# A fused two-attention block: chunks of 128 tokens split into halves of 64, with a state between the halves

## The chip, the cores and the metric

One core of a Trainium2 chip runs the whole program. The metric is the time of one execution in microseconds, the median of the runs.

## The reference, cut to what matters

The input is 4 sequences of 2048 tokens with 512 channels, in float32. Four layers follow one another, each on a layer-normalised copy of x, and each added to x:

```python
x = x + attn_a(layernorm(x))      # causal linear attention, 16 heads of 64
x = x + ffn(layernorm(x), rhs)    # x quantised by rows, rhs by columns, 512x512
x = x + attn_b(layernorm(x))      # gated decaying state, 16 heads, rank 16 x 32
x = x + ffn(layernorm(x), rhs)
```

Attention A takes q = relu(x Wq) + 0.001 and k = relu(x Wk) + 0.001; for each head, the output at token t is q_t times the sum over all tokens up to t of k v, divided by q_t times the sum of k; then Wo and a bias. Attention B turns q and k by a rotary table, projects them by head to rank 16, gates k by a sigmoid, and for each head keeps a 16x32 state M with M = M * decay + k v and y = q M; then an output projection, a residual and a layernorm of its own. Both are sums over all earlier tokens, so they can be worked in chunks: what came before a chunk is a state, and what lies inside it is a masked score matrix.

## The kernel before, in words

**Tiling.** The 8192 tokens are 64 chunks of 128 tokens. A chunk passes through all four layers. Sums over the tokens before a chunk are kept in `state_a` (eight pairs of heads, 64 rows for each head of a pair, 64 columns and one for the sum of k) and in `state_b` (32 rows for each pair of heads).

**Steps.** The kernel is a list of some 95 steps for a chunk, `ORDER`, with a lag for each. The body of the loop is one slot: in slot s a step with lag l works on chunk s - l, and every engine walks the list in this order and does the steps that are its own. So each engine's queue is fixed by the list, up to six chunks are in flight (the largest lag is 5), and engines meet at semaphores only. The first slots, before the loop, also hold the pieces that load, scale and split the weights (`LATE` says after which step), and the last slots drain the pipeline. `BANK` gives each PSUM result one of 8 banks; a bank has a semaphore for full and one for empty, and a step that takes a bank waits until the last user's copy out of it is done.

**TensorE's steps.** Projections are three f16 passes (`three_pass`, L752 to L754: high by high, high by low, low by high): `qk0` to `qk3`, `v0`, `v1`, `wo0`, `wo1`, `qb`, `kb`, `vb`, `gb`, `qr`, `kr`. `mm0` and `mm1` are the two ffn products (L917), `out` is the f32 output projection of attention B (L1038), `kt0`, `kt1`, `kT` are f32 transposes by an identity (L710). The rest are f32 matmuls on parts of the 128x128 array:

- `s0`, `s1` (L832): scores k q of attention A, in blocks of 64 keys by 64 queries, one quarter of the array each. Of the four blocks of a 128x128 score matrix three are computed: the two on the diagonal and the one below it. Places of the halves are swapped for some heads (`key_half`, `query_half`), so that the two row halves of the array have equal work.
- `so0`, `so1` (L847): the queries times `state_a`, started into the banks of o.
- `oa`, `ob` (L870): scores times values, added to the same banks, in two parts with the row halves swapped, so that only one row half of the array writes a bank at a time; `ob` waits for the end of `oa` of its group, with the other group's `oa` between.
- `u0`, `u1` (L889): k transposed times v over all 128 tokens, what the chunk adds to `state_a`.
- `sb` (L990): scores of attention B on tiles of 32 rows by 64 columns, again three blocks of four; `ys` (L1000): the queries times `state_b`, directly behind; `yb` (L1013): values times the 128x128 scores, 128 rows by 32 columns; `ub` (L1026): what the chunk adds to `state_b`.

**Other engines.** VectorE masks the scores on the way out of PSUM (`s_e` L1332, `sb_e` L1470), divides o (`o_e` L1343 to L1353), adds u to the state (`u_e` L1364), makes statistics, normalises (L1285 to L1293) and takes low parts (L1313: the f32 rows less their f16 high part). ScalarE copies v, k transposed and y out and takes high parts; `kT_e` (L1138) copies k transposed of attention B for sb. GpSimd has the powers for the standard deviations, the additions of biases and residuals, and the update of `state_b` (`ub_a` L688, L690). SyncE issues loads, stores and the transposing DMAs (L539): `aT0_t`, `aT1_t` turn the two halves of the divided attention output for `wo0` and `wo1`.

On TensorE the order in the loop is: kt1, v1, kt0, gb, vb, so0, so1, oa1, oa0, ob1, ob0, u1, u0, kb, qb, qk0, qk1, qk2, mm0, kr, mm1, qr, qk3, kT, wo0, sb, ys, wo1, v0, ub, yb, s1, s0, out.

Of the kernel before, what the change touches and what calls it, by code (L numbers as in the profile page):

```python
# [16 lines left out]
P = 128  # L17
# [19 lines left out]
def key_half(pair, place):  # L37
    return place ^ (pair & 1)


def query_half(pair, place):
    return place ^ (pair >> 1 & 1)


def half_of(n):
# [15 lines left out]
ORDER = [("v0_e", 2), ("kt1", 2), ("s1_e", 2), ("v1", 2), ("kt1_e", 2), ("nf0_rs", 3), ("kt0", 2), ("na_rs", 1),  # L61
         ("gb", 4), ("na_ap", 1), ("xTa_h", 1), ("s0_e", 2), ("vb", 4), ("out_e", 5), ("no_st", 5),
         ("no_rs", 5), ("xTa_l", 1), ("so0", 2), ("no_ap", 5), ("ub_a", 5), ("nf0_ap", 3), ("v1_e", 2),
# [11 lines left out]
         ("xTb_h", 3), ("xTb_l", 3), ("ub_e", 4), ("ld_x", 0), ("nf0_st", 2), ("xhb", 4), ("na_st", 0),  # L75
         ("y_e", 4), ("xTb_t", 3), ("x2l", 4), ("out", 4)]
# [6 lines left out]
BANK = {"v0": 7, "v1": 7, "qk0": 5, "qk1": 6, "qk2": 3, "qk3": 6, "kt0": 0, "s0a": 4, "s0b": 3, "o0a": 3, "o0b": 4,  # L83
        "u0": 1, "kt1": 0, "s1a": 5, "s1b": 2, "o1a": 5, "o1b": 6, "u1": 7, "wo": 3, "mm0": 4, "qb": 2, "kb": 0,
        "vb": 2, "gb": 1, "qr": 5, "kr": 0, "sb0": 2, "sb1": 4, "sb2": 5, "sb3": 0, "y0": 1, "y1": 6, "ub": 0,
        "out": 6, "mm1": 2}
BANKS = 8
TAKES = {"s0a": "s0", "s0b": "s0", "s1a": "s1", "s1b": "s1", "o0a": "so0", "o0b": "so0", "o1a": "so1", "o1b": "so1",
         "wo": "wo0", "y0": "sb", "y1": "sb", "sb0": "sb", "sb1": "sb", "sb2": "sb", "sb3": "sb"}
# [3 lines left out]
def taken_by(unit):  # L93
# [11 lines left out]
    (1, "ld_t"): ("load o",),  # L105
    (1, "qk0_e"): ("max o",),
    (1, "kb_l"): ("turn decay",),
    (1, "mm1_e"): ("all o", "keep decay"),
    (1, "sb"): ("scale o", "hi o"),
    (1, "ub"): ("lo o", "load rhs", "load bk"),  # L110
    (2, "gb"): ("max rhs", "all rhs"),
    (2, "no_ap"): ("columns of rhs", "rows of rhs"),
    (2, "ub_a"): ("scale rhs",),
# [169 lines left out]
def hybrid_kernel(nc, x, Wq, Wk, Wv, Wo, bo, q_w, k_w, v_w, g_w, g_b, logits, out_w, out_b, ln_g, ln_b,  # L283
                  rhs, ranks, tables, keeps, out):
    ctx = ExitStack()
    with ctx:
# [420 lines left out]
        def _(pe):  # L707
# [76 lines left out]
            def halves_swapped(x):  # L784
                return x.rearrange("p (h t) -> p h t", h=2)[:, ::-1, :]
# [820 lines left out]
```

## Time and profile before

| | before |
|---|---|
| times of 3 runs | 3124.5, 3125.68, 3126.15 us |
| median | 3125.68 us |
| span of the profiled execution | 3127.1 us |
| mean granted TensorE clock | 0.986 of full speed |
| TensorE, matmuls busy | 3004.2 us (96%) |
| VectorE busy | 2367.4 us (76%) |
| GpSimd busy | 1044.8 us (33%) |
| ScalarE busy | 744.8 us (24%) |

The span goes from the first to the last instruction of the program. Busy is the time in which at least one instruction of the engine runs. Matmuls overlap: each has a duration from its start to its end, and the next starts before that, so what a run of matmuls costs is read from the starts, not from the durations. Each f32 matmul stands in the trace as two instructions.

### The profile page before, as it was taken

How to read it: one execution, taken by the hardware profiler on the slowest of the kernel's cores; microseconds unless marked ns; L12 is line 12 of the kernel's file. 1: busy time of each engine (PE TensorE's matmuls, PEld its weight loads, DVE VectorE, ACT ScalarE, POOL GpSimd, SP SyncE). 2: the span in 40 equal slices, each digit the busy share in tenths (PEclk: the TensorE clock that was granted, in tenths of full speed). 3: DMA queues.
4: the chain of work that ended last, by engine and by line, in shares of the span. 5: the costliest groups of instructions: out<-in, count | busy, mean ns of one | idle time of the engine just before them, and what ended most of it. 6: DMA issues, size and time to landing. Idle time of an engine off the chain costs nothing.

```text
span 3127.1 us, 126889 instructions
## 1 busy us (share of the span) xinstructions
PE 3004.2 (96%) x54866; PEld 2270.9 (73%) x54932; DVE 2367.4 (76%) x5409; ACT 744.8 (24%) x1357; POOL 1044.8 (33%) x1398
## 2 busy tenths in 40 slices
PE   3699999999999999999999999999999999999995
PEld 2577777777777777777777777777777777777663
DVE  6867777777777777777777777777777777777775
ACT  2222222222222222222222122222222222222211
POOL 2023333333333333333333333333333333333333
PEclk9799999999999999999999999999999999999997
DMA  5212222222232222322222222222222222222210
GB/s 173 67 39 49 44 45 51 42 50 46 42 51 44 46 48 46 50 42 47 49 42 48 48 46 45 48 45 45 51 43 49 47 42 51 44 46 48 46 40 24
DMA packets 384396, 153.91 MB, mean 49 GB/s; under 512 B 352800, under 2 KB 361632, under 8 KB 383904
## 3 DMA queue, kind: packets, MB, share of 16 engines
q1 hardware_dynamic: 383904, 146.02, 24.8%
q8 instruction: 471, 7.72, 1.0%
q14 instruction: 21, 0.17, 0.0%
HBM read 45.29 MB, written 16.78 MB: 20 GB/s over the span
## 4 chain that ended last, share of the span: by engine, by line
PE 93%; DVE 4%; issue 1%; DMA 1%; ACT 0%; POOL 0%; SPq 0%; DVEq 0%; POOLq 0%; ACTq 0%
PE bank L752 22%; PE bank L753 21%; PE bank L754 21%; PE bank L1038 8%; PE bank L917 3%; PE bank L832 3%; PE bank L870 3%; PE bank L990 2%; PE bank L710 2%; PE bank L847 2%; PE bank L889 2%; PE bank L1013 2%; PE bank L1000 1%; DVE absmax L1177 1%; PE bank L1026 1%
## 5 line engine op out<-in xcount | busy, mean ns | idle before, releaser
L672 POOL TENSOR_TENSOR work<-work 128x512 f32<-128x512 f32 x128 | 185.6, 1450 | 659.2 <-DVE work L1433 659.2
L752 PE MATMUL bank<-xaT,wq_hi 128*128 128x128 f16 x2048 | 359.9, 220 | 6.3 <-DVE wk_lo L1202 4.0
L753 PE MATMUL bank<-xaT,wq_hi 128*128 128x128 f16 x2048 | 359.9, 220 | 0.0
L754 PE MATMUL bank<-xaT,wq_lo 128*128 128x128 f16 x2048 | 359.9, 220 | 0.0
L752 PE MATMUL bank<-xaT,wk_hi 128*128 128x128 f16 x2048 | 358.8, 220 | 0.0
L753 PE MATMUL bank<-xaT,wk_hi 128*128 128x128 f16 x2048 | 358.6, 220 | 0.0
L754 PE MATMUL bank<-xaT,wk_lo 128*128 128x128 f16 x2048 | 358.5, 220 | 0.0
L752 PE MATMUL bank<-xbT,wb 128*128 128x128 f16 x2048 | 348.3, 220 | 0.0
L753 PE MATMUL bank<-xbT,wb 128*128 128x128 f16 x2048 | 347.6, 219 | 0.6 <-issue 0.6
L754 PE MATMUL bank<-xbT,wb 128*128 128x128 f16 x2048 | 347.5, 219 | 0.0
L1322 DVE TENSOR_SCALAR work<-bank,eps_q 128x256 f32<-128x256 f32 x256 | 123.0, 481 | 178.7 <-PE bank L754 178.7
L1470 DVE TENSOR_TENSOR work<-bank,causal 128x512 f32<-128x512 f32 x256 | 158.8, 682 | 117.2 <-PE bank L990 117.1
L1038 PE MATMUL bank<-wout,work 128*128 128x512 f32 x512 | 242.6, 617 | 2.7 <-ACT work L1151 2.7
L695 POOL TENSOR_TENSOR xf<-xwb,xf 128x512 f32<-128x512 f32 x64 | 81.5, 1274 | 438.6 <-DVE xf L1410 438.6
L1138 ACT ACTIVATE work<-bank,odd_even 128x256 f32<-128x256 f32 x128 | 53.6, 470 | 645.5 <-PE bank L710 645.5
L752 PEld LDWEIGHTS bank<-xaT,wq_hi 128*128 128x128 f16 x2048 | 201.7, 99 | 7.2 <-issue 4.3
L752 PEld LDWEIGHTS bank<-xbT,wb 128*128 128x128 f16 x2048 | 200.7, 98 | 4.5
L753 PEld LDWEIGHTS bank<-xaT,wq_hi 128*128 128x128 f16 x2048 | 201.7, 98 | 0.2
L754 PEld LDWEIGHTS bank<-xaT,wq_lo 128*128 128x128 f16 x2048 | 201.8, 99 | 0.0
L753 PEld LDWEIGHTS bank<-xbT,wb 128*128 128x128 f16 x2048 | 200.9, 98 | 1.0 <-issue 0.7
L752 PEld LDWEIGHTS bank<-xaT,wk_hi 128*128 128x128 f16 x2048 | 201.4, 98 | 0.0
L753 PEld LDWEIGHTS bank<-xaT,wk_hi 128*128 128x128 f16 x2048 | 201.4, 98 | 0.0
(210 smaller groups left out, 8243.0 us busy)
## 6 DMA issues: line engine op xcount, KB each, us to landing
xin<-in_L_attn_a_x SPq DMA_DIRECT2D x64, 256.0 KB, 2.6
out<-xf SPq DMA_DIRECT2D x64, 256.0 KB, 2.1
table<-in_tables SPq DMA_DIRECT2D x64, 192.5 KB, 2.6
work<-in_L_attn_a_Wq SPq DMA_DIRECT2D x1, 2048.0 KB, 7.9
work<-in_L_attn_a_Wk SPq DMA_DIRECT2D x1, 2048.0 KB, 12.9
wb<-in_L_attn_a_Wv SPq DMA_DIRECT2D x1, 2048.0 KB, 17.6
work<-in_L_attn_a_Wo SPq DMA_DIRECT2D x1, 2048.0 KB, 8.4
work<-work SPq DMA_TRANSPOSE x128, 3.9
```

The costliest lines, as they stand in the source:

```text
L672: pool.tensor_tensor(to[:, :, :, :], to[:, :, :, :], cross[:, :, ::-1, :], ALU.add)\
L695: pool.tensor_tensor(xf1[:, :], xwb[:, c.par, :], xf1[:, :], ALU.add)\
L710: last = nc.tensor.transpose(bank[:, i * P:(i + 1) * P], src(i), id_)
L752: nc.tensor.matmul(o, a[0], b[0], start=first, stop=False)
L753: nc.tensor.matmul(o, a[0], b[1], start=False, stop=False)
L754: return nc.tensor.matmul(o, a[1], b[0], start=False, stop=last)
L832: last = nc.tensor.matmul(bank[half_of(place), at:at + HALF], qk[half_of(p), 1, m, half_of(place)], qk[half_of(p), 0, m, half_of(q)], star ...
L870: last = nc.tensor.matmul(bank[half_of(place_q), i * VA:(i + 1) * VA], sc[g][half_of(place_k), p, i, half_of(q)], va[half_of(place_k), 2 * ...
L917: last = nc.tensor.matmul(bank[:, :], xqT[w][:, k, :], rhs_q[:, k, :], start=k == 0, stop=k == KD - 1)
L1038: last = nc.tensor.matmul(bank[:, :], yT[:, k, :], wout[:, k, :], start=k == 0, stop=k == KD - 1)
L1322: last = nc.vector.tensor_scalar(qk[:, n, m, :].rearrange("p m t -> p (m t)"), bank[:, 256 * n:256 * n + 256], 0.0, e_[:, :], ALU.max, ALU ...
L1470: nc.vector.tensor_tensor(scb[:, l, :, :].rearrange("p (j o) t -> p j o t", j=2), bank[:, :].rearrange("p (j o t) -> p j o t", j=2, o=2), ...
```

## The change

Each chunk is worked in two halves of 64 tokens.

- **Attention A.** `u(g)` computes what each half adds, into two banks (`u0a`, `u0b`); `u_e(g)` makes `middle_a` = state + first half's sum, and the next chunk's state from it with the second. The state is double (`state_a[:, par]`). `so(g)` multiplies the first half's queries by the state and the second half's by `middle_a`. Then only the two diagonal 64x64 blocks are left: one step `s` for all eight pairs of heads into two banks, and one step `o(g)` for each group in place of `oa` and `ob`. In a bank of o, both row halves of the array now write, to different partitions; `o(g)` first waits for the end of `so(g)` (`so_done`).
- **Attention B.** The same: `sb_` computes diagonal blocks alone, `ub` makes two sums, `ub_m` (GpSimd) makes `middle_b`, `ub_a` the next state. `ys` becomes two steps, `ys0` and `ys1`, which write both banks of y from the two halves in turn; `ys1` waits for `ys0`. `yb` runs on 64 rows by 32 columns.
- The swapped places of halves go, and with them the split copies of v, o, k of B and the masks for them.
- `ORDER`, `BANK`, `LATE`, `BORROWED` and the table of wait counts are new. The largest lag is 4. The weight pieces stand in slots 0 to 2 (before: 1 to 3), the load of out_w comes last among them, and g's, rk's and rq's weights are staged in its buffer. Some tiles share memory otherwise (`xf1` and `vbs` are now parts of `work`), and small ones are parts of one.

On TensorE the order in the loop is now: vb, mm1, qr, kT, ub, mm0, sb, so1, o1, ys0, ys1, yb, wo0, out, wo1, kb, qb, qk0, qk2, qk1, v1, v0, kt0, qk3, gb, u0, s, kt1, kr, so0, u1, o0.

The core of the diff:

```diff
-            def s(g):
-                    heads = range(4 * g, 4 * g + 4)
-                    places = [shares(place, lambda m: (0, 1), heads) for place in range(2)]
...
+            def s(c):
+                pair = c.take_behind(("s_a", "s_b"), [(f"qk{i}", 0) for i in range(4)])
+                waited()
+                for m in range(PAIRS):
+                    for h in range(2):
+                        for p, (bank, f) in enumerate(pair):
+                            last = nc.tensor.matmul(bank[half_of(h), HALF * m:HALF * m + HALF], qk[half_of(p), 1, m, half_of(h)],
+                                                    qk[half_of(p), 0, m, half_of(h)], start=True, stop=True,
+                                                    skip_group_check=True)
...
+                    for i in range(4):
+                        m = 4 * g + i
+                        for h, state in enumerate((state_a[:, c.par, :, :], middle_a[:, :, :])):
+                            for p, (bank, _) in enumerate(pair):
+                                last = nc.tensor.matmul(bank[out_half(p, h), i * VA:(i + 1) * VA],
+                                                        qk[half_of(p), 0, m, half_of(h)], state[half_of(p), m, :],
+                                                        start=i == 0, stop=False, skip_group_check=True)
+                                if i == 3 and h == 1:
+                                    last.then_inc(so_done[g], 1)
...
+            def o(g):
+                def step(c):
+                    c.take_behind((), [(n, 0) for n in ("v0", "v1", "s_a", "s_b")])
+                    c.wait(so_done[g], c.count(0, 2))
+                    waited()
+                    pair = [c.bank(f"o{g}{n}") for n in "ab"]
+                    for i in range(4):
+                        m = 4 * g + i
+                        for p, (bank, f, _) in enumerate(pair):
+                            for h in range(2):
+                                last = nc.tensor.matmul(bank[out_half(p, h), i * VA:(i + 1) * VA], sc[g][half_of(h), p, i, :],
+                                                        va[half_of(h), 2 * m + p, :], start=False, stop=i == 3,
+                                                        skip_group_check=True)
...
+                            for h, (bank, f) in enumerate(two):
+                                last = nc.tensor.matmul(bank[half_of(p), i * VA:(i + 1) * VA],
+                                                        ktok[half_of(h), n * DA:(n + 1) * DA], va[half_of(h), n, :],
+                                                        start=True, stop=True, skip_group_check=True)
...
+            def ys(swap):
+                def step(c):
+                    if swap:
+                        two = [c.bank(f"y{h}")[0] for h in range(2)]
+                        c.wait(ys_begun, c.count(0, 4))
...
+                            h = g // 2 ^ swap
+                            state = middle_b[:, :, :] if h else state_b[:, c.par, :, :]
+                            rows = slice(32 * g, 32 * g + 32)
+                            last = nc.tensor.matmul(two[h][half_of(g % 2), at_y(2 * j + g // 2)], state[rows, j, :],
+                                                    qh[rows, j, half_of(h)], start=swap == 0 and j == 0, stop=False,
+                                                    skip_group_check=True)
...
+                        for h, (bank, f, _) in enumerate(two):
+                            last = nc.tensor.matmul(bank[l * DB:(l + 1) * DB, at_y(b)], vbs[half_of(h), n * DB:(n + 1) * DB],
+                                                    scb[half_of(h), n % 8 // 2, 2 * (n // 8) + n % 2, :], start=False,
+                                                    stop=b == BB - 1, skip_group_check=True)
...
+            def ub_m(c):
+                c.done("ub0")
+                c.wait(b_ready, c.count(1))
+                c.all_filled(("y0", "y1"), 1)
+                pool.tensor_tensor(middle_b[:, :, :], state_b[:, c.par, :, :],
+                                   decay64[:, :, None].to_broadcast([P, 2, 2 * DB]), ALU.mult).then_inc(b_faded, 1)
+                c.wait(b_faded, c.count())
+                pool.tensor_tensor(middle_b[:, :, :], middle_b[:, :, :], u_tmp[:, 0, :, :], ALU.add)\
+                    .then_inc(middle_ready, 1)
...
+                    nc.vector.tensor_tensor(middle, state_a[:, c.par, m, :].rearrange("p m e -> p (m e)"), bank[:, 0:4 * VA],
+                                            ALU.add).then_inc(e, 1)
+                    bank, e = c.read(f"u{g}b")
+                    c.done(f"u{g}a")
+                    nc.vector.scalar_tensor_tensor(state_a[:, 1 - c.par, m, :].rearrange("p m e -> p (m e)"), middle,
+                                                   keep_a[:, c.par, 1:2], bank[:, 0:4 * VA], ALU.mult, ALU.add).then_inc(e, 1)
```

## Rows read from the trace of the kernel before

**Rows 1.** The page, busy us (share of the span) and instructions of an engine.
```profile
PE 3004.2 (96%) x54866; PEld 2270.9 (73%) x54932; DVE 2367.4 (76%) x5409; ACT 744.8 (24%) x1357; POOL 1044.8 (33%) x1398
```

**Rows 2.** Windows: stretch, us, busy (count) of each engine, PEclk, DMA share, GB/s.
```profile
2024.70:2071.12 46.42, 46.37 (x861) 35.14 (x858) 35.66 (x84) 11.21 (x21) 16.11 (x21) 1.00 0.28 46
...
0.00:150.00 150.00, 72.28 (x1134) 57.24 (x1135) 111.85 (x184) 35.71 (x30) 20.18 (x63) 0.84 0.38 122
2977.00:3127.00 150.00, 113.14 (x1769) 78.44 (x1771) 94.72 (x196) 25.83 (x52) 54.37 (x68) 0.88 0.14 32
```

**Rows 3.** The page's chain that ended last, share of the span by engine.
```profile
PE 93%; DVE 4%; issue 1%; DMA 1%; ACT 0%; POOL 0%; SPq 0%; DVEq 0%; POOLq 0%; ACTq 0%
```

**Rows 4.** Timeline of TensorE in one period: start, us, engine, line, operation, shapes, count.
```profile
2013.62 0.39 PE L710 MATMUL bank<-ident,work 128*128 128x128 f32 x2
...
2016.53 1.20 PE L990 MATMUL bank<-work 32*64 32x64 f32 x92
...
2017.59 0.65 PE L1000 MATMUL bank<-work,state_b 32*64 32x128 f32 x14
2018.18 0.39 PE L752 MATMUL bank<-wo_hi,work 128*128 128x512 f16 x1
...
2023.15 0.38 PE L754 MATMUL bank<-wv_hi,xaT 128*128 128x512 f16 x1
2023.46 0.43 PE L1026 MATMUL bank<-vbs,work 128*32 128x64 f32 x16
2023.71 1.06 PE L1013 MATMUL bank<-work,vbs 128*32 128x128 f32 x32
2024.70 1.63 PE L832 MATMUL bank<-work 64*64 64x64 f32 x96
2026.26 3.70 PE L1038 MATMUL bank<-wout,work 128*128 128x512 f32 x8
...
2036.76 0.38 PE L753 MATMUL bank<-wb,xbT 128*128 128x512 f16 x1
2036.98 0.38 PE L754 MATMUL bank<-wb,xbT 128*128 128x512 f16 x1
2037.29 1.22 PE L847 MATMUL bank<-state_a,work 64*64 64x65 f32 x64
2038.30 1.66 PE L870 MATMUL bank<-va,work 64*64 64x65 f32 x96
2039.89 1.15 PE L889 MATMUL bank<-va,work 128*64 128x65 f32 x32
2040.97 0.23 PE L752 MATMUL bank<-xbT,wb 128*128 128x128 f16 x1
```

**Rows 5.** Timeline, kT of the next chunk on TensorE and the copies behind it.
```profile
2060.13 0.39 PE L710 MATMUL bank<-ident,work 128*128 128x128 f32 x2
...
2060.63 0.84 ACT L1138 ACTIVATE work<-bank,odd_even 128x256 f32<-128x256 f32 x2 [10.41 <-PE bank L710]
```

**Rows 6.** Timeline of VectorE: the first eviction of s0 in this period.
```profile
2026.39 0.69 DVE L1332 TENSOR_TENSOR work<-bank,causal 128x512 f32<-128x512 f32 x1 [0.39 <-PE bank L832]
```

**Rows 7.** Groups of VectorE, 1500 to 2475 us: form, count, busy us, mean ns, idle before.
```profile
L1353 DVE TENSOR_TENSOR work<-bank,recip_d 64x128 f32<-64x128 f32 x168 | 48.5, 289 | 2.3
...
L1364 DVE SCALAR_TENSOR_TENSOR state_a<-state_a,keep_a,bank 128x260 f32<-128x260 f32 x42 | 19.9, 474 | 0.0
...
L1453 DVE TENSOR_TENSOR work<-bank,q_decay 128x256 f32<-128x256 f32 x21 | 8.6, 411 | 0.0
```

**Rows 8.** Single lines, 1500 to 2475 or 2460 us: statistics, subtraction, landing of transposing DMAs.
```profile
L1285 DVE BATCH_NORM_STATS2 stats_b<-xwb 128x6 f32<-128x512 f32 x21 | 14.4, 686 | 0.0
...
L1313 DVE TENSOR_TENSOR work<-work x40: 680/1219/1764, 1536.5 to 2420.1; 128x512 f16<-128x512 f32 x40
...
DMA to landing us min/median/max: 2.5/3.3/4.9
```

More of the change, by code:

```diff
@@ L104 @@
 LATE = {
[L105 to L113, printed above, removed]
-    (2, "nf1_st"): ("max bk", "all bk"),
-    (2, "vb_e"): ("scale bk", "hi bk"),
-    (2, "kb_a"): ("round rhs", "load bq"),
-    (2, "qk0_e"): ("lo bk", "load g", "load rk", "load rq"),
@@ new lines @@
+    (0, "aT1_h"): ("load rk",),
+    (0, "aT1_l"): ("load rq",),
+    (0, "qk3"): ("max o", "all o"),
+    (0, "qk2_e"): ("scale o",),
+    (0, "s_e"): ("hi o",),
+    (0, "u1"): ("lo o",),
+    (1, "aT0_h"): ("load rhs",),
+    (1, "vb_e"): ("turn decay",),
+    (1, "qT0_t"): ("keep decay",),
+    (1, "mm0_e"): ("load bk",),
+    (1, "ld_t"): ("max rhs",),
+    (1, "st_o"): ("max bk",),
+    (1, "bias"): ("all rhs",),
+    (1, "no_rs"): ("all bk",),
+    (1, "wo_e"): ("columns of rhs", "load g"),
@@ new lines @@
+    (1, "nf1_st"): ("rows of rhs",),
+    (1, "kb_e"): ("scale rhs", "scale bk"),
+    (1, "nf1_ap"): ("round rhs",),
+    (1, "qk0"): ("load bq",),
+    (1, "rnd1"): ("hi bk",),
+    (1, "nf0_q"): ("lo bk",),
+    (1, "u0_e"): ("max bq",),
+    (1, "o0"): ("max g",),
+    (2, "aT0_h"): ("all g",),
+    (2, "mm0_e"): ("max rk",),
+    (2, "mm0_a"): ("all bq",),
+    (2, "aT1_h"): ("max rq",),
+    (2, "nb_ap"): ("scale bq",),
+    (2, "na_rs"): ("scale g", "hi bq"),
+    (2, "bias"): ("hi g", "all rk"),
@@ new lines @@
+    (2, "wo1"): ("lo bq",),
+    (2, "no_ap"): ("scale rk",),
+    (2, "x2l"): ("hi rk",),
+    (2, "wo_e"): ("lo g",),
+    (2, "kb_e"): ("lo rk",),
+    (2, "nf1_ap"): ("all rq",),
+    (2, "nf0_ap"): ("load bv",),
+    (2, "qk0"): ("scale rq",),
+    (2, "nf1_q"): ("hi rq", "max bv"),
+    (2, "xhb"): ("all bv", "lo rq"),
+    (2, "rnd1"): ("scale bv",),
+    (2, "qT1_t"): ("hi bv",),
+    (2, "qk2_e"): ("lo bv",),
+    (2, "u0"): ("load wout",),
+}
+TAKEN = ("q", "k", "v", "o", "rhs", "bk", "bq", "g", "rk", "rq", "bv")
@@ new lines, in at_y @@
+            def at_y(b):
+                return slice(HALF * b, HALF * b + HALF)
+            def ys(swap):
[3 more added lines that the diff above has]
+                        c.wait(ys_begun, c.count(0, 4))
+                    else:
+                        two = [c.take(f"y{h}")[0] for h in range(2)]
+                        c.done("qr")
+                        c.wait(b_ready, c.count(1))
+                        c.wait(middle_ready, c.count())
+                    waited()
+                    for j in range(2):
+                        for g in range(4):
+                            h = g // 2 ^ swap
[4 more added lines that the diff above has]
+                                                    skip_group_check=True)
+                            if swap == 0 and j == 1:
+                                last.then_inc(ys_begun, 1)
+                return step
@@ L1004, in yb @@
             def yb(c):
-                two = [c.bank("y0"), c.bank("y1")]
+                two = [c.bank(f"y{h}") for h in range(2)]
                 c.done("vb")
@@ L1019, in ub @@
             def ub(c):
-                bank, f = c.take("ub")
+                two = [c.take(f"ub{h}") for h in range(2)]
                 c.wait(khat_ready, c.count())
                 c.done("vb")
+                waited()
                 for j in range(2):
                     for g in range(4):
-                        h = 8 * j + 2 * g
-                        last = nc.tensor.matmul(bank[32 * g:32 * g + 32, 64 * j:64 * j + 64],
-                                                khat[:, h * R:(h + 2) * R], vbs[:, h * DB:(h + 2) * DB],
-                                                start=True, stop=True, skip_group_check=True)
@@ L1029, in ub @@
-                last.then_inc(f, 1)
+                        n = 8 * j + 2 * g
+                        for h, (bank, f) in enumerate(two):
+                            last = nc.tensor.matmul(bank[32 * g:32 * g + 32, 64 * j:64 * j + 64],
+                                                    khat[half_of(h), n * R:(n + 2) * R], vbs[half_of(h), n * DB:(n + 2) * DB],
+                                                    start=True, stop=True, skip_group_check=True)
+                            if j == 1 and g == 3:
+                                last.then_inc(f, 1)
```

490 lines of the change are left out of this document (207 added, 283 removed), and 57 rows, old and new, of tables (COUNTS, LATE, ORDER).

## The prediction

> **What bounds the kernel now.** The page's busy shares come first: TensorE 96% of a span of 3127.1 us, VectorE 76% [rows 1]. A share is an average, so the next view is a stretch out of the steady loop, about a period long: TensorE is busy 46.37 of 46.42 us, VectorE 35.66, GpSimd 16.11, with the granted clock at 1.00, so 2.4 GHz [rows 2]. The chain that ended last says the same: 93% of it is TensorE, 4% VectorE [rows 3]. In the loop a microsecond of TensorE work is a microsecond of time, and nothing else is late. The period follows from the two transposes of kT, which start at 2013.62 and 2060.13: 46.5 us for a chunk [rows 4, 5], 64 × 46.5 = 2976 us. The other 151 us are start and drain: in the first 150 us TensorE is busy 72.3, in the last 150 it is busy 113.1 [rows 2].
>
> **What the change does to TensorE's stream.** Only the f32 steps on small tiles change; the projections, the transposes, wo, out and mm keep their columns and counts. One f32 matmul stands as two instructions in the trace. The cost of a step is read from the timeline as the start of the next section less its own start [rows 4]: sb with ys 2016.53 to 2018.18, 1.65; ub 0.25; yb 0.99; s 1.56; so 1.01; o 1.59; u 1.08 us. Together 8.13 us of the 46.5.
>
> Inside these lie switches between shapes. The last 128x512 matmul ahead of a small-tile section holds TensorE 0.31 us (2023.15 to 2023.46, 2036.98 to 2037.29), where the one before it took 0.22 (2036.76 to 2036.98) [rows 4]. A switch of shape is 0.09 us. I take the same for every change of tile shape: I count 3 on the way in and 5 on the way from a shape to another or out, in the order sb,ys | ub,yb,s | so,o,u. Pure streaming is then: s 1.47, o 1.50, so 1.01, u 0.99, sb with ys 1.56, ub 0.25, yb 0.90, sum 7.68.
>
> After the change, in instructions for a chunk:
> - s goes from 96 to 64, same shape: 1.47 × 2/3 = 0.98. o likewise: 1.00. so keeps 64: 1.01.
> - u goes from 32 of 128*64 to 64 of 64*64 with the same columns, which is so's form: 1.01.
> - sb goes from 96 to 64. Its stretch to the first long one of ys is 1.06 us, 11 ns each [rows 4]: 0.70. ys has 32 of 64 columns for 16 of 128: what is left of 1.56, 0.50.
> - yb goes from 32 of 128*32 with 128 columns to 64 of 64*32 with 64 columns, ub from 16 of 128*32 to 32 of 64*32. Eight tiles at once is a form the trace has only in sb (32*64). Bounds: twice as fast as s's four tiles, 7.7 ns, or no faster than s, 15.3 ns. I take sb's 11 ns, the nearest row: yb 0.70, ub 0.35.
>
> Sum 6.25, so 1.43 us less. The bounds on eight tiles move it by -0.3 and +0.4.
>
> What is added on TensorE's own queue:
> - Three more switches of shape. The new order is ub | mm0 | sb, so1 o1, ys0 ys1, yb | ... u0 s | kt1 kr | so0 u1 o0 |. That makes 11 shape changes for 8: +0.27. A page of the Trainium skill bears on it: "TensorEngine Tiling (Array Packing)", Key Properties, says that changing the tiling mode, not just the tile, drains the engine. The trace agrees, with 0.09 us; were the drain free, the period would be 0.27 shorter still.
> - Two waits of TensorE for itself with nothing between: o1 waits for the end of so1, ys1 for the end of ys0. Everything on TensorE queues behind them. (o0's wait for so0 has u1's 0.5 us as cover.) The trace has no such wait in the loop. Nearest: s's last matmul starts about 0.15 before the out projection at 2026.26, and VectorE, which waits for it, starts at 2026.39 [rows 4, 6], so 0.28 from the start of the last to the waiter; a weight load follows. Bounds 0.13 (2026.39 less 2026.26) and 0.50 (kT's start at 2060.13 to ScalarE's at 2060.63 [rows 5]). I take 0.30 each: +0.60.
>
> The net is -1.43 + 0.27 + 0.60 = -0.56 us for a chunk, × 64 = -36 us.
>
> **Beside TensorE.** VectorE loses 2 of 4 evictions of s at 0.69 [rows 6], the four of sb, of s's shape now, go to the 0.41 of the 128x256 row, o's twelve at 0.29 become six at about 0.41, kr_e's three at 0.29 one at 0.41; it gains two of u at 0.47 and one ub at 0.29 [rows 7]: -1.38 -1.12 -1.02 -0.46 +0.94 +0.29 = -2.75 us, to 32.9 of 46. ScalarE drops the split copies of v and vb. GpSimd gains two passes over the 128x128 state, some 1.2 us on 16.1. None becomes the bound by its sum, so these edits cost nothing as long as TensorE hides them. Three chains come close instead:
> - kT to sb. Now kT starts at 2060.13 and its copies end at 2061.47 [rows 5], with wo0's 2.6 us as cover. In the new order kT 0.22, ub 0.35, mm0 0.86 (four steps of 0.22) and two switches are all: 1.61 against 1.34 plus a hand-over. Margin about 0.2.
> - sb to yb. sb 0.70, 0.28 to the waiter, four evictions at 0.41: 2.6 from sb's start. TensorE's own path with both waits is 3.1. If the self-waits were free, about 0.5 could be given back, 0.6 not.
> - o1 to wo1. From sb's start, o1 is visible at 2.4; o1_e (two reciprocals and three of about 0.41, behind sb_e) ends at 4.2, nb_st's statistics and two short ones at 5.1; the 128x512 subtraction behind ScalarE's copy, at its short 0.68, ends near 6.1, and the transposing DMA lands 3.3 later at its median [rows 8]: 9.4. TensorE comes to wo1 at 3.9 (yb's end) + 2.6 (wo0) + 3.6 (out) = 10.1. Margin 0.7. In the kernel before, these stand far ahead of wo0: TensorE waits for neither in the loop, as its 46.37 busy of 46.42 shows.
>
> **Start and drain.** The largest lag falls from 5 to 4, so one slot less of a part-filled pipeline; the weight pieces move into slots 0 to 2, and the load of out_w goes to the end of them. The work in them is the same. In the drain the last chunk runs a chain of the same steps. I take -3 us, bounds -20 and +15, as the 78 us idle at the start and the 37 at the end [rows 2] are waits that mostly stay.
>
> **Sum.** 3127.1 - 36 - 3 = 3088 for the span. The runs' median, 3125.7, is 1.4 below the profiled span, so the prediction is 3087 us, 1.2% faster.
>
> **The rivals.**
> - Free waits and full eight-tile rate (chance 0.2). yb and ub at 7.7 ns, self-waits at 0.13: -1.73 + 0.27 + 0.26 = -1.2 us × 64 = -77, about 3045. For it: the waits may run while earlier tiles still stream. Against: sb itself does not reach twice s's rate [rows 4].
> - No change (0.05). Self-waits at 0.50 and ub, yb at 15 ns: -1.03 + 0.27 + 1.0 = +0.2, 3125 with a little help from the drain. Against: both bounds at once.
> - Slower by the new place of wo1 (0.12). o1_e, nb_st, the copy, the subtraction and the transpose stand in a row before wo1, and out alone covers the last. The subtraction takes 0.68 to 1.76 us, the DMA 2.5 to 4.9 [rows 8]. With 1.76 and 3.9 for 0.68 and 3.3, wo1 starts 1.0 late in each chunk: 3087 + 64 × 1.0 = 3151. It turns the sign when wo1 is over 0.6 late. Against: the longest landings belong to pairs issued together, which the new order separates.
> - Slower by the banks (0.03). In o both halves of the key rows now write one bank at the same time, to different partitions. If that made them take turns, o's 1.00 becomes 2.00: +64, 3151. Against: ys does just this now, two row groups into one bank, and its 16 instructions of 128 columns take about 0.50 us, where yb's 32, four tiles at once, take 0.90 [rows 4]: 0.5 is the rate of four at once; two would be 0.9. The page just named states the rule, under Gotcha 1: PSUM Pressure (different row tiles cannot access one bank simultaneously); ys's row speaks against it for separate partitions.
> - That the work is not cut as the text says has nothing for it: the blocks are counted by the loops.
>
> **How the numbers follow.** Forecast 0.6, the rivals 0.2, 0.05, 0.12 and 0.03. About 0.2% is what a measurement of this kernel can tell from no change. Faster: 0.6 + 0.2, of which a little touches zero, 0.80. Same: 0.05. Slower: 0.15. The range leaves out the far end of the wo1 case and the best tenth of the fast one: 3040 to 3140.
>
> **What would show it.** A period of 45.9 us, against 45.3 in the fast case and over 46.6 in the slow. s and o shorter by a third, sb near 0.70, yb and ub near 11 ns an instruction. A gap of 0.3 us ahead of the first matmul of o1 and of ys1. TensorE idle ahead of wo's second half would show the wo1 rival; o at twice its per-instruction time the banks. The prediction is wrong if the period is outside 45.4 to 46.6, or if start and drain move by more than 20 us.

## The result, and the profile after

The changed kernel takes 3302.48 us (median of 4 runs, 3297.75 to 3305.38); the kernel before, beside it on the same chip, 3125.91. The ratio is 1.0561, 95% interval 1.0547 to 1.0574: 5.6% slower, where 3087 us, 1.2% faster, was forecast, with a range of 3040 to 3140. The profiled execution has a span of 3302.3 us.

First the page of the changed kernel: busy time by engine, the instruction queue (packets, MB, share), the chain that ended last, and one group of costly instructions.

```profile
PE 3054.3 (92%) x54932; PEld 2245.8 (68%) x54932; DVE 2317.0 (70%) x4958; ACT 644.7 (20%) x1165; POOL 1046.3 (32%) x1520
...
q8 instruction: 472, 7.73, 1.0%
...
PE 90%; issue 5%; DVE 3%; DMA 1%; ACT 0%; POOL 0%; POOLq 0%; SPq 0%; DVEq 0%; ACTq 0%
...
L774 PE MATMUL bank<-wb,xbT 128*128 128x512 f16 x256 | 120.2, 470 | 93.2 <-issue 93.2
```

TensorE is busy 50 us longer than before [rows 1] and yet has only 92% of the span. The chain has 5% "issue", where it had 1% [rows 3]: time in which TensorE waits for nothing that the profile shows. The group says where: vb's 128x512 matmuls, 93.2 us idle ahead of them, and 470 ns each, where the same shape takes 387 ns elsewhere on the page (wo).

The period, from one `out` to the next, was 46.4 to 46.5 us in the loop. Now two lengths alternate: 53.05 and 47.26 us. The loop's body holds two slots, so the long one is the period with the back edge, the branch from the body's end to its start. Next, TensorE's timeline of the changed kernel around a back edge (start, us, line, operation, shapes, count, idle before):

```profile
1497.61 0.92 PE L871 MATMUL bank<-va,work 64*64 64x65 f32 x32
1501.88 0.60 PE L774 MATMUL bank<-wb,xbT 128*128 128x512 f16 x1 [3.35 <-issue]
1502.28 0.63 PE L775 MATMUL bank<-wb,xbT 128*128 128x512 f16 x1
```

The last step of the list, o0, ends its small tiles at 1498.5; then TensorE stands still until 1501.88, with the releaser "issue". The control instructions of the loop at this back edge, by the line of the loop (durations in ns, then first and last start):

```profile
L492 PEldq COMPARE_BRANCH  x1: 3373/3373/3373, 1498.2 to 1498.2; - x1
...
L492 DVEq COMPARE_BRANCH  x1: 61/61/61, 1498.9 to 1498.9; - x1
```

And the same instruction in the kernel before:

```profile
L481 PEldq COMPARE_BRANCH  x1: 3199/3199/3199, 2026.1 to 2026.1; - x1
```

TensorE's branch takes 3.4 us here, the branch of VectorE 61 ns. Over all passes its median is 3572 ns after and 3147 before: the branch was as long before the change. It cost nothing there, since it starts at 2026.1, just as `out` begins [rows 4], whose eight f32 matmuls keep the array busy to 2029.96. In the new list it stands behind so0, u1 and o0, 16 to 20 ns a matmul with its load: the last matmul in the queue starts 0.15 us after the branch begins.

Windows of the changed kernel, columns as in [rows 2]: the start, the 2.2 us behind the branch, and a stretch without one.

```profile
0.00:150.00 150.00, 85.85 (x1290) 64.54 (x1291) 118.48 (x190) 33.70 (x30) 27.60 (x67) 0.91 0.45 128
1501.80:1504.00 2.20, 2.12 (x6) 0.74 (x7) 0.00 (x0) 0.00 (x0) 0.00 (x0) 0.50 0.61 70
1550.00:1600.00 50.00, 47.37 (x894) 35.52 (x893) 36.39 (x81) 9.66 (x18) 16.11 (x23) 1.00 0.18 43
```

Behind the gap the granted clock is 0.50, so 1.2 GHz, and six 128x512 matmuls take the whole 2.2 us (0.40 to 0.43 us from start to start); further on it is 1.00. By starts, in medians over the loop, o0 with the gap behind it takes 4.98 us for the 0.63 of its neighbour without one, and vb 4.29 for 2.60: 4.35 + 1.69 = 6.0 us a pass. The loop has 27 passes and its branch is taken 26 times: 157 us.

The rest of the loss is smaller. What TensorE waited for between 1000 and 2500 us (total us, times, longest):

```profile
PE bank L774 <- issue: 53.5, 15, 3.9
PE bank L1007 <- PE bank L1007: 6.6, 30, 0.3
PE bank L871 <- PE bank L853: 6.1, 30, 0.2
PE bank L1007 <- issue: 5.7, 14, 0.8
PE bank L871 <- issue: 4.2, 11, 0.7
PE bank L886 <- issue: 3.3, 9, 0.6
```

The two waits for its own results are as forecast in kind. The three small "issue" rows stand in the middle of ys (L1007), o0 (L871) and u1 (L886), behind no wait at all. The second period in detail:

```profile
1545.98 0.70 PE L886 MATMUL bank<-va,work 64*64 64x65 f32 x32
1546.49 1.11 PE L839 MATMUL bank<-work 64*64 64x64 f32 x64
1547.54 0.66 PE L732 MATMUL bank<-ident,work 128*128 128x128 f32 x4
...
1549.31 0.65 PE L886 MATMUL bank<-va,work 64*64 64x65 f32 x28
1550.22 0.33 PE L886 MATMUL bank<-va,work 64*64 64x65 f32 x4 [0.26 <-issue]
1550.54 0.70 PE L871 MATMUL bank<-va,work 64*64 64x65 f32 x32
...
1555.62 0.45 PE L1039 MATMUL bank<-work 64*32 64x64 f32 x32
1556.00 1.04 PE L915 MATMUL bank<-rhs_q,xqT 128*128 128x512 bf16 x4
1556.97 0.91 PE L983 MATMUL bank<-work 32*64 32x64 f32 x64
1557.81 0.28 PE L853 MATMUL bank<-state_a,work 64*64 64x65 f32 x2
...
1558.71 0.70 PE L871 MATMUL bank<-va,work 64*64 64x65 f32 x32 [0.20 <-PE bank L853]
1559.34 0.27 PE L1007 MATMUL bank<-work,state_b 32*64 32x64 f32 x2
...
1560.06 0.47 PE L1007 MATMUL bank<-work,middle_b 32*64 32x64 f32 x3 [0.26 <-PE bank L1007]
...
1560.64 0.86 PE L1024 MATMUL bank<-work 64*32 64x64 f32 x64
```

u1 stops after 28 of its 32 (0.26 us idle). Counted from the start of TensorE's branch (the last few matmuls, still queued then, are counted too), such stops stand, whenever they come, at the same four instructions, each in 8 to 22 of the 26 passes: 426, 1706, 2218 and 3499, which are 5, 2 and 5 times 256 apart, to within one. The page gives the instruction queue 7.73 MB in 472 packets, 16 KB each. TensorE's 54932 matmuls and as many loads would be 429 packets of 256 instructions; waits and register work bring them to 440, and one packet more at each taken branch gives 466 of the 472. The Trainium skill ("Advanced Engine Details and Errata", ISA Cache) gives a cache line of 16 KB, 256 instructions, and says that there are only two lines; beside this it gives TensorE 128 KB, which would be eight. The packets' size and number agree with the line, and the spacing of the stops with them; how many lines TensorE has, no run here shows.

### The profile page after: what moved, and what is told of

Its sections match the earlier page's. It is cut to its first block, busy times and chain, and to the rows that moved or that the text cites. A ratio compares the mean times of both kernels' runs of the same rounds, so it can differ in the third digit from the quotient of the medians.

```text
span 3302.3 us, 127393 instructions
## 1 busy us (share of the span) xinstructions
PE 3054.3 (92%) x54932; PEld 2245.8 (68%) x54932; DVE 2317.0 (70%) x4958; ACT 644.7 (20%) x1165; POOL 1046.3 (32%) x1520
## 3 DMA queue, kind: packets, MB, share of 16 engines
q8 instruction: 472, 7.73, 1.0%
## 4 chain that ended last, share of the span: by engine, by line
PE 90%; issue 5%; DVE 3%; DMA 1%; ACT 0%; POOL 0%; POOLq 0%; SPq 0%; DVEq 0%; ACTq 0%
PE bank L774 21%; PE bank L775 21%; PE bank L776 21%; PE bank L1052 7%; PE bank L915 4%; PE bank L871 3%; PE bank L853 2%; PE bank L732 2%; PE bank L886 2%; PE bank L1007 2%; PE bank L839 2%; PE bank L1024 2%; PE bank L983 2%; PE bank L1039 1%; DMA work<-work 0%
## 5 line engine op out<-in xcount | busy, mean ns | idle before, releaser
L1330 DVE TENSOR_SCALAR work<-bank,column 128x256 f32<-128x256 f32 x512 | 222.4, 475 | 316.6 <-PE bank L776 316.4
L775 PE MATMUL bank<-xaT,wq_hi 128*128 128x128 f16 x2048 | 358.4, 220 | 0.0
L775 PE MATMUL bank<-xaT,wk_hi 128*128 128x128 f16 x2048 | 356.6, 219 | 0.0
L775 PE MATMUL bank<-xbT,wb 128*128 128x128 f16 x2048 | 346.3, 219 | 0.0
L683 POOL TENSOR_TENSOR work<-work 128x512 f32<-128x512 f32 x128 | 176.9, 1382 | 399.3 <-DVE work L1448 399.3
L656 POOL TENSOR_TENSOR var_eps<-mean_var,column 128x1 f32<-128x1 f32 x320 | 61.3, 191 | 753.2 <-DVE mean_var L1296 750.9
L717 POOL TENSOR_TENSOR work<-xwb,work 128x512 f32<-128x512 f32 x64 | 82.3, 1287 | 633.7 <-DVE work L1425 633.7
L1052 PE MATMUL bank<-wout,work 128*128 128x512 f32 x512 | 232.6, 597 | 1.6 <-ACT work L1153 1.6
L774 PE MATMUL bank<-wo_hi,work 128*128 128x512 f16 x512 | 198.0, 387 | 10.2 <-DMA work<-work 10.1
L774 PE MATMUL bank<-wb,xbT 128*128 128x512 f16 x256 | 120.2, 470 | 93.2 <-issue 93.2
L775 PEld LDWEIGHTS bank<-xbT,wb 128*128 128x128 f16 x2048 | 200.4, 98 | 6.6
L659 POOL TENSOR_TENSOR rstd<-var_eps,column 128x1 f32<-128x1 f32 x320 | 196.3, 613 | 25.0
L1147 ACT ACTIVATE work<-work 128x512 f16<-128x512 f32 x128 | 79.6, 622 | 628.1 <-POOL work L683 628.1
L775 PEld LDWEIGHTS bank<-xaT,wq_hi 128*128 128x128 f16 x2048 | 201.1, 98 | 0.7
```

The source lines that it names most:

```text
L659: pool.tensor_tensor(rstd[n][:, one], var_eps[n][:, one], half[:, :], ALU.pow).then_inc(rs[n], 1)
L683: pool.tensor_tensor(to[:, :, :, :], to[:, :, :, :], cross[:, :, ::-1, :], ALU.add)\
L717: pool.tensor_tensor(xf1[:, :], xwb[:, c.par, :], xf1[:, :], ALU.add)\
L774: nc.tensor.matmul(o, a[0], b[0], start=first, stop=False)
L775: nc.tensor.matmul(o, a[0], b[1], start=False, stop=False)
L1052: last = nc.tensor.matmul(bank[:, :], yT[:, k, :], wout[:, k, :], start=k == 0, stop=k == KD - 1)
```

## The experiments

The seam is the place in the list where the loop's body ends and the branch stands. Theory after the two traces: (1) the seam, TensorE's branch met with an empty queue, makes the large part; (2) the supply of instructions in blocks of 256 makes a smaller part wherever a whole block is small tiles. A stop is idle time of TensorE that no wait explains. Rivals: the small tiles or their waits are slow in themselves; the clock falls because of them. All moved seams keep every engine's instructions in their order. In the kernels made from the changed one most lines stand one later: ys is L1008, yb L1025, o L872, u L887, mm L916, so L854, the first of three passes L775. Seam_after_vb keeps the old numbers.

**1. seam_after_out.** The list begins elsewhere, lags and due slots carried along:
```diff
-ORDER = [("u1_e", 1), ("aT0_h", 1), ("vb", 3), ... ("out", 3), ("xTb_h", 2), ... ("o0", 0), ("o0_e", 0)]
+ORDER = [("xTb_h", 3), ... ("o0", 1), ("o0_e", 1), ("u1_e", 1), ("aT0_h", 1), ("vb", 3), ... ("out", 3)]
```


> The changed kernel with the same instructions in the same order on every engine; only the place where the loop's body ends is moved, from behind o0 (small tiles) to behind out, where it stood in the kernel before. Theory (seam): what made the change slow is PE's branch at the back edge (median 3.57 us), which the changed kernel meets with a drained queue, so that PE stands 3.7 us and goes on at 1.2 GHz; behind out, eight matmuls of 427 ns stand in the queue and cover it. The two slow sections cost 4.36 us (o0) and 1.69 us (vb) per pass of the loop, 27 passes: 3302 - 163 = 3139 us, 3125 to 3155; o0 goes from 4.98 to about 0.63 us in every period, and no period is 53 us. Rival (instruction supply or waits of the small tiles themselves): the time stays within 20 us of 3302. Rival (the clock falls because of the small tiles): the gap goes, the 1.2 GHz steps stay, 3200 us.

3187.22 us (3172.79 to 3193.85), ratio to before 1.0202 [1.0185, 1.0219]: 115 us of the 177 are gone, with nothing changed but the seam and what moves with it. o0 takes 0.63 us in the median of either half of the body, and vb's matmuls behind it keep to 216 ns, so the small tiles alone do not bring the clock down. But 48 us more than expected stay. Its waits, 1000 to 2500 us, and one yb in its timeline:

```profile
PE bank L1025 <- issue: 26.8, 30, 2.1
...
PE bank L775 <- issue: 1.7, 5, 0.4
```

```profile
1594.81 0.66 PE L1025 MATMUL bank<-work 64*32 64x64 f32 x40
1597.02 0.43 PE L1025 MATMUL bank<-work 64*32 64x64 f32 x24 [1.54 <-issue]
```

Ahead of the three passes, where the changed kernel had 53.5 us of this kind, there are 1.7. yb stops after 40 of its 64, with nothing to wait for. Moving the seam changed how many instructions stand ahead of the loop, and so where the borders of 256 fall: now at 1669 and 3461, both in yb. In the profiled executions a pass of two chunks goes from 100.50 to 95.40 us, 5.1 less: 6.0 for the seam, less 0.9 by which the stops have grown (0.8 us a period before, 1.25 now, both over the 46.45 of a period without seam and stops). So the missing part is mostly the stops. The rest is spread from run to run: the profiled execution, at 3172.79, was the fastest of the four, 14 us under their median.

**2. before_seam_after_u.** The kernel before, with its seam behind u0:
```diff
-ORDER = [("v0_e", 2), ... ("u0", 2), ("kb", 4), ... ("out", 4)]
+ORDER = [("kb", 4), ... ("out", 4), ("v0_e", 1), ... ("u0", 1)]
```


> The kernel before the change, same instructions in the same order; only the end of the loop's body is moved, from behind out to behind u0, so that the 64-wide steps of s, o, u stand ahead of PE's branch, as in the changed kernel. Theory (seam): the branch takes 3.15 us as before but is exposed now, and the steps behind it run at 1.2 GHz for a while; 4.5 to 6 us per pass, 27 passes: 3126 + 120 to 165 = 3245 to 3290 us. Rival (the seam is harmless, the change's own small tiles are what costs): 3126 us within 10.

3339.53 us, 1.0684 [1.0667, 1.0702]. The unchanged work, with its seam in such a place, is slower than the changed kernel. With experiment 1 this leaves nothing large for the rival that the change's own tiles are slow.

```profile
PE bank L750 <- issue: 53.7, 15, 4.0
PE bank L868 <- issue: 16.0, 15, 1.4
PE bank L887 <- issue: 14.7, 15, 1.3
```

53.7 us ahead of kb in 15 passes is the seam, as in the changed kernel (53.5). The other two rows are supply stops in o (L868) and u (L887), at instructions 1703 and 3496, 7 times 256 apart; I had not counted on them. They are 51 us of idle time over the loop, some 60 from start to start, and they are why it exceeds the range.

**3. seam_after_vb.** The changed kernel, seam behind vb, the list beginning with `("mm1", 4)`.

> The changed kernel, same order, with the end of the loop's body behind vb: twelve matmuls of 216 ns (2.6 us) ahead of PE's branch instead of out's eight of 427 ns (3.43 us). Theory (the queue covers the branch only as long as what stands in it lasts): the queue holds fewer microseconds of work, so part of the 3.57 us stays exposed, 0.8 to 2.5 us per pass, with little of the slow clock: 3139 + 25 to 65 = 3160 to 3205 us. Rival (it matters only whether large tiles stand ahead): as with the seam behind out, 3139 within 10.

3202.58 us, 1.0249 [1.0232, 1.0266], inside the range, but not by the seam alone:

```profile
PE bank L915 <- issue: 16.3, 15, 1.3
PE bank L871 <- issue: 11.2, 25, 0.9
PE bank L1007 <- issue: 11.2, 20, 0.8
```

Twelve 216 ns matmuls leave 1.1 us a pass idle (16.3 in 15) of 3.7: what is queued covers the branch for as long as it lasts. That is 27 us over the loop, as the theory has it; the other two rows are supply stops, which the expectation had left out, so that the total fell into the range by luck. By these three seams the exposed time is about 0 behind 3.4 us of queued work, 1.1 behind 2.6, and 3.6 behind 0.15.

**4. before_moved_196.** Theory (2) alone, on the kernel before:
```diff
-            pe.wait_ge(s_pool, 9)
+            for _ in range(394):
+                pe.wait_ge(s_pool, 9)
```
(Two such waits go into one instruction.)

> The kernel before the change, with 196 more PE instructions ahead of its loop and none in it: waits on a semaphore that already has its value, in the stretch in which PE has nothing to do but wait for its first weights. Theory (PE's instructions are fetched in blocks of 256, one block ahead, and a block is usable some 3.1 to 3.9 us after the block before it was entered): in the loop only the places of the block borders move, 196 instructions earlier; a whole block then lies inside the 384 dense instructions of s, o, u (1.88 us for 256) in both halves of the body, entered too late to be covered by the queued 216 ns matmuls: two stalls of 1.0 to 1.6 us per pass, 27 passes, 3126 + 55 to 80 = 3180 to 3205 us, all of it in gaps without a wait, 256 x n instructions apart. Rival (the stalls seen with the moved seam belong to the place of the seam or to o and u themselves): 3126 within 8.

3182.07 us (3181.05 to 3184.01), 1.0179 [1.0162, 1.0196]. Nothing inside the loop differs, and it is 55 us slower. A pass takes 94.78 us for 92.98, 49 us over the loop; the rest lies outside it, where the first `out` starts 11 us later.

```profile
PE bank L870 <- issue: 20.2, 15, 1.7
```

The stop stands in o at instruction 2202 (the theory's count gave 2213) in each of the 25 passes between two branches, 1.56 us from start to start on average. I had expected one in the other half of the body as well; there the loss is only 0.1 us. The kernel as it was has a block of 1.85 us too, but there a packet of the instruction queue starts 2.2 us (median) before the array enters that block, under vb's queued 128x512 matmuls, and not 0.9 us after it as here.

**5. waits_covered.** From here on the seam is behind out. Other matmuls stand ahead of both self-waits; mm1 comes from behind vb and takes bank 4, and its eviction by VectorE moves with it:
```diff
-("sb", 3), ("so1", 1), ("o1", 1), ... ("ys0", 3), ("sb_e1", 3), ("ys1", 3)
+("sb", 3), ("so1", 1), ("mm1", 4), ("ys0", 3), ("o1", 1), ... ("ys1", 3)
```


> The changed kernel with the loop's end behind out, and on PE the order so1, mm1, ys0, o1, ys1 instead of mm1 early and so1, o1, ys0, ys1: each of the two waits of PE for its own stop (0.42 us ahead of o1, 0.40 us ahead of ys1) has other matmuls queued in front of it. Theory: both waits are gone but for the switches of shape that the new order adds (four at about 0.09): 0.45 to 0.65 us per chunk, 64 chunks, 29 to 42 us below the run with the seam behind out, so about 3105 us. Rival (something else is late at the same place, such as instruction supply or the state's halves): under 10 us below it.

3400.8 us, 1.0875 [1.0856, 1.0893]: 296 above the expected 3105.

```profile
PE bank L1008 <- issue: 46.9, 15, 3.2
PE bank L1008 <- POOL middle_b L702: 46.2, 14, 3.3
```

Both rows are one wait of 3.2 us ahead of ys0; the second names it, the middle state of GpSimd. GpSimd's timeline shows why:

```profile
1500.01 1.29 POOL L718 TENSOR_TENSOR work<-xwb,work 128x512 f32<-128x512 f32 x1 [11.07 <-DVE work L1426]
1501.27 0.39 POOL L699 TENSOR_TENSOR middle_b<-state_b,column 128x128 f32<-128x128 f32 x1
1501.73 0.45 POOL L702 TENSOR_TENSOR middle_b<-middle_b,u_tmp 128x128 f32<-128x128 f32 x1
```

L718 is the addition behind mm1. It had stood ahead of the middle state at no cost; with mm1 moved, it waits for mm1's eviction, and ys0 waits behind it.

**6. waits_covered_pool.** On GpSimd, `("mm1_a", 4)` goes behind `("ub_m", 3)`.

> As waits_covered, with one thing changed: on GpSimd the addition behind mm1 (1.3 us, which waits for mm1's eviction by DVE at L1426) stands behind the middle state's two steps and not ahead of them. Theory: the 3.66 us that PE stood ahead of ys0 in each chunk came only from that order; they go, and with them the two self-waits (0.42 and 0.40 us per chunk), and mm1's 1.7 us inside the dense run of sb, so, ys, o, yb give the fetch of the next block the time that it lacked ahead of yb (0.8 us per chunk): against the run with the seam behind out, -26 to -90 us, 3097 to 3160, my value 3115. Rival (the middle state is late by its own inputs, the scores' copies or the state's matmuls): a gap of over 0.5 us stays ahead of ys0, 3160 us or more.

3134.44 us (3128.24 to 3142.54), 1.0026 [1.0011, 1.0040]. Both self-waits are gone from the view, and the gap ahead of ys0 too:

```profile
PE bank L1025 <- issue: 21.8, 20, 2.0
PE bank L775 <- issue: 1.0, 3, 0.4
```

Against seam_after_out that is 53 us less. It is the fastest form of the change that these runs have, 168 us under the changed kernel and still 0.3% above the kernel before; no run beats that one.

**7. Places of the borders.** waits_covered_pool with 85, 149 and 181 more TensorE instructions ahead of the loop (as in experiment 4, `range(172)`, `range(300)`, `range(364)`).

> waits_covered_pool (hint kept) with 85 more PE instructions ahead of its loop. Theory (a stall comes where 256 instructions take PE less than the 3.7 to 3.9 us that the next block needs): the borders stand 85 instructions earlier; by the trace of waits_covered_pool the shortfall per pass is 1.06 to 1.86 us there, against 0.5 to 0.9 at the present place: 15 to 30 us more, 3145 to 3165, and no stall at instruction 1669 or 3461 of the body. Rival (place matters, but not by this sum): outside 3140 to 3170. Rival (place is no matter): 3134 within 5.

> The same with 149 instructions. The shortfall by the sum is 0.4 to 0.6 us per pass: 3125 to 3135 us. Rivals as for 85.

> The same with 181 instructions. The shortfall by the sum is 0.15 to 0.55 us per pass, the smallest of all places: 3115 to 3130 us, below the kernel before in the best case. Rivals as for 85.

Measured 3152.16 (ratio 1.0092 [1.0075, 1.0109]), 3134.93 (1.0032 [1.0021, 1.0043]) and 3199.56 (1.0238): the first two in their ranges, the third 70 us above its own. The stops moved as the theory wants: 1072 and 2864 with 85; 2800 and 3313 with 149, so 64 instructions earlier for 64 more ahead of the loop. Their sizes don't follow my sum: with 181, stops of 1.0 us in mm1 and 1.6 to 1.8 in yb, from start to start, stand where the sum had almost nothing. The waits with 149:

```profile
PE bank L887 <- issue: 10.2, 16, 0.8
PE bank L775 <- DMA work<-work: 7.5, 12, 1.4
PE bank L872 <- issue: 4.7, 10, 0.6
```

yb is free, u1 and o are not, and a transfer of aT1 has become late (work<-work), of which more in experiment 10. TensorE's branch itself is shorter here; with 85:

```profile
L493 PEldq COMPARE_BRANCH  x26: 88/1850/2318, 643.8 to 3018.0; - x26
```

It is 1.85 us with 85 and 1.92 with 149, but 3.26 in waits_covered_pool and 3.57 with 181. The instruction queue shows the difference. With 181 and in the changed kernel one 16 KB packet starts inside each taken branch, 1.0 us in; with 85 and 149 it starts ahead of the branch. In all four the branch ends 1.2 to 1.6 us after that packet has landed. So the place of the borders sets the length of the branch too.

**8. The hint.** Without `hint_back_edge=True`, one instruction less at the head of TensorE's body (`BRANCH_PREFETCH_HINT` in the trace, by its name a notice of the coming branch).

> The changed kernel without the hint to the instruction fetch that stands at the head of its loop (one PE instruction less per pass). If the 3.57 us of PE's branch are the fetch of the body's first block, and the hint, 3,500 instructions earlier, has no effect left when the branch comes: 3302 within 10, the branch takes 3.2 to 3.9 us still. Rival (the hint shortens it): 10 to 80 us more.

> The kernel before the change without the hint at the head of its loop. Theory (the hint delays the branch's first block by some 0.5 us, as the changed kernel lost 0.68 us per odd period with it, and out's queue hides the branch here): within 6 of 3127. Rival (the hint hides part of the branch, which out's eight matmuls cover only just): 5 to 30 us more.

> As waits_covered_pool, without the hint at the head of the loop. In waits_covered_pool the only idle time of PE left is the supply of yb (median gap 0.78 and 1.6 us in the two halves of the body) and a branch now and then exposed. Theory (the hint makes the fetch near the loop's end and the branch slower, 20 us in the changed kernel): 3134 - 10 to 25 = 3109 to 3124 us. Rival (the 20 us came from the exposed seam alone): 3134 within 5.

The changed kernel gets faster, which neither theory expected: 3282.11, 20 us less. The branch's median is 3.55 us for 3.57; the idle time ahead of vb falls by 4 us and that of the stops by 11. The kernel before gets slower, 3158.65, ratio 1.0105 [1.0090, 1.0121], and so does the covered one, 3158.43. For the kernel before the rival was right in kind, 32 us more where it had 5 to 30, and by the branch (min, median, max ns):

```profile
L481 PEldq COMPARE_BRANCH  x26: 83/4638/5059, 630.7 to 2987.8; - x26
```

4.64 us for 3.15 with the hint, more than `out` covers. In each of these branches the instruction queue has two packets where it had one with the hint; in the changed kernel it has one with and without. My reading from the changed kernel alone was wrong.

**9. covered_moved_242.** covered_no_hint with `range(486)` waits.

> As covered_no_hint, and with 242 more PE instructions (satisfied waits) ahead of the loop, which puts the block borders 14 instructions later in the body: the blocks that end in yb then hold more of the slow matmuls ahead of sb. By the time from one border to the next of the trace, against the 3.7 to 3.9 us that a block seems to need, the shortfall goes from 0.5 to 0.9 us per pass to 0.25 to 0.45: 7 to 15 us less than covered_no_hint, 3100 to 3115 us. Rival (the position within a block is no matter, or the shortfall has another size): within 4 of covered_no_hint.

3197.47, 1.0231 [1.0217, 1.0244]: 39 us more, not 7 to 15 less. The stop in yb moved by 16 instructions where it should by 14, and a new one of 1.9 us idle stands in so1, a border ahead of it.

**10. wo0_split.** On waits_covered_pool, the two short blocks are made longer; `parts` is (0, 1) in wo0 and (2, 3) in wo0r:
```diff
-("ys1", 3), ... ("yb", 3), ... ("wo0", 1), ("y_e", 3)
+("ys1", 3), ("wo0", 1), ... ("yb", 3), ("wo0r", 1), ... ("y_e", 3)
-                    for i in range(4):
+                    for i in parts:
```


> waits_covered_pool with the first six of wo0's twelve matmuls (216 ns each) ahead of yb and the other six behind it; nothing else changes, and the body has the same number of PE instructions. Theory (a block of 256 that PE runs through faster than its successor comes makes the stall at instruction 1669 and 3461, in yb): the blocks that end there get 1.3 us more work, against stalls of 0.8 and 1.6 us: the idle time in yb (40 us between 500 and 2900 us) goes to under 10: 3134 - 25 to 50 = 3084 to 3109 us, my value 3095, which is below the kernel before. Rival (yb's result, which out needs, loses half of wo0 as cover, or aT0's transposes come too late for wo0's earlier half): a gap of 0.3 us or more ahead of out or wo0 in each chunk, 3110 to 3140. Rival (the supply is late by a fixed rhythm and not by short blocks): the stall stays in yb, 3134 within 8.

```profile
PE bank L775 <- DMA work<-work: 12.3, 13, 2.0
PE bank L775 <- DMA xbT<-work: 8.6, 10, 1.1
PE bank L1025 <- issue: 5.2, 10, 0.9
```

3145.75, 1.0050 [1.0037, 1.0064]. The stop in yb falls from 21.8 to 5.2 us per 1500, as forecast, and the time does not follow: wo1 now waits for the transposes of aT1 (DMA work<-work, 12.3) and kb for xbT (8.6). Those waits were 0.0 and 0.2 in waits_covered_pool. What the supply gave back, the next late transfers took. The recorded rival had a late transfer, but ahead of wo0 or out.

## Why the prediction was wrong

By its own steps:

- **"In the loop a microsecond of TensorE work is a microsecond of time, and nothing else is late."** Right for the kernel before, and the step that failed for the new one. The prediction summed sections of matmuls and never asked what TensorE's sequencer does at the loop's end, although the diff moves it. Experiments 1 to 3 show what stood in its place: the branch, 3.15 us and hidden under `out` before, 3.57 us and exposed now, with 1.2 GHz behind it. It is worth 157 us by the sections; experiment 1 gained 115 net, as the stops in yb came with the new place of the borders.
- **Supply.** Not in the prediction at all. In the changed kernel the stops add about 0.8 us to a period by starts (50.25 as the loop's mean, less 3.0 for the seam and 46.45 without either), some 40 us over the loop. Experiment 4 shows that the kernel before is free of it only by the place of its borders.
- **s 0.98, ub 0.35, yb 0.70.** s 1.04 in the median, ub 0.39 and yb 0.79 with their switches: right. **o likewise by a third:** no. Cut into two steps of 32 matmuls, o is 2 x 0.63 for 1.58: -0.33 for -0.5. **sb with ys:** 0.84 + 0.78 for 0.70 + 0.50. A step of few tiles pays its entry each time, which the rate of a long stretch does not show.
- **Self-waits, 0.30 each.** They are there, 0.42 ahead of o1 and 0.40 ahead of ys1 from start to start: within the bounds, 0.22 too small together.
- **Net -0.56 us for a chunk.** The sections' differences, without seam and stops, add up to -0.02: -0.84 of streaming and switches, +0.82 of self-waits. So the part that it did model for the loop was wrong in size too: it gives no gain.
- **Start and drain, -3.** The first `out` starts at 178.0 us where it was 210.8; start and drain together are about 28 us shorter (175 more in the span, 203 of it in the loop's 54 chunks). In the first 150 us TensorE is busy 85.9 us for 72.3 [rows 2]. This is outside the bound of 20 given, and not the -3 of the sum. Had the branch been covered and no stop come, the loop's -1 and these -28 would make about 3098 by this estimate, inside the range, but by two errors that cancel: the gain would have come from the start and not from the chunks.
- **The wo1 rival, margin 0.7.** It did not decide the result, but it is what comes next: L775 of wo1 waits for aT1's transposes in 149 and in wo0_split, as soon as TensorE arrives a microsecond earlier.
- **The banks rival** has nothing for it: o takes 19.6 ns a matmul, entry included, where it took 16.5, and not twice as much.

What stays open: how long a block must last. Stops came after blocks of 1.9 to 3.3 us, but not after every such block, and moving the borders by 32 instructions from 149 to 181 cost 65 us. That a late packet makes the stops is argued from their spacing and from experiment 4, which moves nothing else in the loop. A packet mostly starts within 2 us of the moment when the array crosses a border, before it or behind; what holds some up longer the runs don't tell. Nor is it shown why the hint saves a packet and 1.5 us in the branch behind `out` and neither in the one behind o0.

## What to carry to other kernels

In a loop whose body is thousands of instructions on TensorE, look where the back edge stands: put it behind the slowest matmuls, and read the branch's own record and the "issue" share of the chain before and after any reordering. In these runs 3.4 us of queued matmuls covered a branch of up to some 3.5 us, and not one of 4.6. Where small tiles run at 16 to 20 ns a matmul with its load, count instructions as well as columns: 256 instructions, some 1.9 us, could pass faster than the next 256 came (experiment 4), so try long matmuls between dense steps. It is no sure gain: the finer sums of experiments 7, 9 and 10 all missed somewhere. A chain moved on one engine drags its followers on the others; read each engine's order past the moved step before the sum is made.

## What the hardware showed beyond that

- A taken branch costs TensorE 3.15 us (kernel before) and 3.57 us (after) in the median, and the other four engines 49 to 61 ns in the changed kernel, with the same loop line. Over all runs TensorE's median goes from 1.85 us (covered_moved_85) to 4.9 us (covered_no_hint), with the work of the loop all but the same. The last, untaken branch takes TensorE 88 ns. The Trainium skill gives one figure and names no engine ("Advanced Engine Details and Errata", Control Flow Timing: compare-and-branch about 108 ns). The untaken branch and the other engines are below it; TensorE's taken one, in a body of some 3,500 instructions, is about 30 times as long.
- 196 idle instructions ahead of a loop made its unchanged passes 1.9% longer (experiment 4).
- A gap of 3.4 us was followed by vb's matmuls at 427 ns from start to start, at a granted clock of 0.50. Gaps of 0.6 to 2.7 us in yb, in seam_after_out, were followed by 128x512 matmuls at 216 ns in 28 cases of 33 and at 427 in five.
